# Splitting the second convolution's weights in the second stage, slab by slab, with ACT and GpSimd instead of VectorE

## The reference, cut to what matters

```python
def _dcnv2(x, w_off, b_off, w, b, k, pad):
    om = conv(x, w_off) + b_off                 # offsets and a gate for each tap of each pixel
    sy, sx = offsets + pixel grid + tap grid
    mask = sigmoid(om[:, 2 * P:])
    val = _bilinear(x, sy, sx) * mask           # four neighbours, weighted
    return einsum('ncphw,ocp->nohw', val, w) + b

h = _bn_lrelu(_dcnv2(x, w_off1, b_off1, w1, b1, 1, 0), ...)   # 512 -> 256 channels, 1 tap
h = _bn_lrelu(_dcnv2(h, w_off2, b_off2, w2, b2, 3, 1), ...)   # 256 -> 512 channels, 9 taps
return x + h
```

## Time and profile before

| | us |
|---|---|
| median of 3 runs | 3176.06 (3172.43 to 3177.47) |
| the profiled execution | 3181.72 |
| its span on the core | 3179.9 |
| mean granted TensorE clock | 0.984 of full speed |

### The profile page before, as it was taken

The page is one execution under the profiler, slowest core; times in us unless marked ns, Lnnn a source line. Parts: engine busy times, 40 slices in busy tenths (PEclk is TensorE's granted clock), DMA queues, the critical chain, the costliest instruction groups (busy, mean ns, idle before and its releaser), DMA issues.

```text
span 3179.9 us, 52201 instructions
## 1 busy us (share of the span) xinstructions
PE 3045.7 (96%) x15660; PEld 2472.5 (78%) x15660; DVE 2755.8 (87%) x4830; ACT 2510.6 (79%) x4736; POOL 1681.7 (53%) x1701
## 2 busy tenths in 40 slices
PE   6997888989999999999999999999999999999998
PEld 6997445558888888888888888888888888888888
DVE  5545899978999998998999998999989999999987
ACT  3665677778888888888888888888888888888886
POOL 0001444456656666566566666566666665666652
PEclk8999899989999999999999999999999999999999
DMA  8998999999999999999999999999999999999994
GB/s 310 322 339 299 352 349 332 334 332 398 373 357 378 368 362 376 365 365 379 359 370 377 357 372 374 356 381 367 359 379 363 364 368 350 362 362 352 367 347 174
DMA packets 432939, 1124.82 MB, mean 354 GB/s; under 512 B 42908, under 2 KB 173084, under 8 KB 432848
## 3 DMA queue, kind: packets, MB, share of 16 engines
q0 software_dynamic: 244672, 891.09, 75.1%
q1 hardware_dynamic: 116944, 161.19, 14.4%
q10 hardware_dynamic: 71232, 71.57, 6.5%
HBM read 1003.70 MB, written 137.04 MB: 359 GB/s over the span
## 4 chain that ended last, share of the span: by engine, by line
PE 69%; DVE 17%; issue 6%; ACT 5%; DMA 2%; ACTq 1%; DVEq 0%; SPq 0%; POOLq 0%
PE psum_t L1269 49%; PE psum_t L1256 9%; PE psum_t L386 5%; PE psum_t L697 4%; DVE arena L1190 4%; DVE val_first L1198 2%; DVE z_sb L1212 2%; DVE val_lo L1205 2%; DVE arena L835 1%; ACT val_hi L1153 1%; ACT psum_t L1139 1%; DMA arena<-w 1%; ACT z_sb L1162 1%; PE psum_t L682 1%; DVE arena L859 1%
## 5 line engine op out<-in xcount | busy, mean ns | idle before, releaser
L1125 POOL DMA_INDIRECT arena<-table,plan_in x1521 | 1516.2, 997 | 968.6 <-DVE arena L1198 419.0
L1269 PE MATMUL psum_t<-val_hi,w_hi 128*128 128x512 f32 (+2 forms) x3096 | 1240.4, 401 | 1.8 <-ACT z_sb L1162 0.5
L1269 PE MATMUL psum_t<-val_hi,w_lo 128*128 128x512 f32 (+2 forms) x3096 | 1200.2, 388 | 0.0
L1269 PE MATMUL psum_t<-val_lo,w_hi 128*128 128x512 f32 (+2 forms) x3096 | 1196.8, 387 | 0.0
L1139 ACT ACTIVATE psum_t<-arena,plan_in 128x512 f32<-128x512 f32 x1521 | 1044.1, 686 | 138.2 <-DVE arena L1190 133.9
L1190 DVE SCALAR_TENSOR_TENSOR arena<-arena,plan_in,psum_t 128x512 f32<-128x512 f32 x1521 | 1123.1, 738 | 10.6 <-ACT psum_t L1139 10.5
L1269 PEld LDWEIGHTS psum_t<-val_hi,w_hi 128*128 128x128 f32 x3096 | 582.6, 188 | 137.2 <-ACT z_sb L1162 36.2
L1269 PEld LDWEIGHTS psum_t<-val_hi,w_lo 128*128 128x128 f32 x3096 | 581.7, 188 | 121.1
L1205 DVE TENSOR_TENSOR val_lo<-psum_t,val_hi 128x1024 fp32r<-128x1024 f32 (+2 forms) x387 | 465.4, 1203 | 230.4 <-ACT val_hi L1153 230.3
L1269 PEld LDWEIGHTS psum_t<-val_lo,w_hi 128*128 128x128 f32 x3096 | 583.7, 189 | 102.9
L1153 ACT ACTIVATE val_hi<-psum_t 128x1024 fp32r<-128x1024 f32 (+2 forms) x387 | 390.0, 1008 | 281.2 <-PE psum_t L1256 281.0
(11 more groups left out here) (90 smaller groups left out, 2454.7 us busy)
## 6 DMA issues: line engine op xcount, KB each, us to landing
arena<-x SPq DMA_DIRECT2D x90, 512.0 KB, 8.3
table<-arena ACTq DMA_DIRECT2D x42, 896.0 KB, 8.3
out<-arena SPq DMA_DIRECT2D x136, 256.0 KB, 4.7
table<-arena ACTq DMA_DIRECT2D x42, 768.0 KB, 7.1
arena<-x SPq DMA_DIRECT2D x70, 384.0 KB, 6.3
arena<-table,plan_in POOLq DMA_INDIRECT x1521, 6.7
table<-table SPq DMA_DIRECT2D x32, 512.0 KB, 8.8
arena<-w POOLq DMA_DIRECT2D x2, 2304.0 KB, 13.9
```

The lines of the kernel that those rows point to most:

```text
L1125: nc.gpsimd.indirect_dma_start(landing(r, i)[:, :], None, rows, bass.IndirectOffsetOnAxis(ap=row.bitcast(u32), axis=0))\
L1269: last = nc.tensor.matmul(psum_acc[:, oc, 0:n], a[:, w, oc * P:(oc + 1) * P], b[:, r % 2, kt, 0:n], start=(w == 0 and a is w2_hi and b is ...
```

## The change

1. The two DMAs of nine slabs, the wait between them, and `split_w2` leave the first stage. DVE's program there is `lower` for every tile, and the plan.
2. A new buffer `w2_slab` of 128 x 512 holds one raw slab. In the second stage SP loads two slabs at the start of its step of chunks 0 to 8, each after the split of the slab before it.
3. ACT makes the high part of slab 2c in its step of tile 13c + 19, and of slab 2c + 1 in that of tile 13c + 25, after the folds.
4. POOL makes the low part nine tiles later in its own order, before the gather of tile 13c + 28 or 13c + 34. It waits for ACT's high part.
5. POOL no longer waits for the slabs before its first gather. PE waits for all of them at the second stage's end.

```diff
+SPLIT_AT = (19, 25)
+SPLIT_LAG = 9
...
-                pool.wait_ge(w1_scaled, 1)
-                for part_no in range(2):
-                    if part_no:
-                        pool.wait_ge(w2_split, HALF_SLABS)
-                    pool.dma_start(w2_raw, w2[part_no * HALF_SLABS * P:(part_no + 1) * HALF_SLABS * P, :]
-                                   .rearrange("(s p) n -> p s n", p=P)).then_inc(raw_loaded[part_no], 16)
...
-                    if s == 0:
-                        dve.wait_ge(raw_loaded[part_no], 16)
-                    hi, lo = w2_hi[:, slab, :], w2_lo[:, slab, :]
-                    link(nc.vector.tensor_copy(hi, w2_raw[:, s, :]))
-                    nc.vector.tensor_tensor(lo, w2_raw[:, s, :], hi.bitcast(f32), ALU.subtract)\
-                        .then_inc(w2_split, 1)
...
                 for c in range(CHUNKS):
                     n = plan_tiles(c)
+                    for slab in slabs_of(c):
+                        if slab:
+                            sp.wait_ge(w2_split, slab)
+                        sp.dma_start(w2_slab[:, :], w2[slab * P:(slab + 1) * P, :]).then_inc(w2_loaded, 16)
                     sp.wait_ge(chain2, (c + 1) * (CHAIN + 1))
...
-                pool.wait_ge(w2_split, SLABS)
+                def lower_w2(slab):
+                    pool.wait_ge(w2_hi_ready, slab + 1)
+                    nc.gpsimd.tensor_tensor(w2_lo[:, slab, :], w2_slab[:, :], w2_hi[:, slab, :].bitcast(f32),
+                                            ALU.subtract).then_inc(w2_split, 1)
+
                 pool.wait_ge(chain1, PLAN_STEPS_1)
                 for t in range(TILES):
+                    if split_at(t - SPLIT_LAG) is not None:
+                        lower_w2(split_at(t - SPLIT_LAG))
...
                 pe.wait_ge(gate_ready, CHUNKS)
+                pe.wait_ge(w2_split, SLABS)
...
+                def upper_w2(slab):
+                    act.wait_ge(w2_loaded, (slab + 1) * 16)
+                    nc.scalar.activation(w2_hi[:, slab, :], w2_slab[:, :], ACT.Identity).then_inc(w2_hi_ready, 1)
...
                     for dy in range(3):
                         if t - 7 - dy in BAND_AT:
                             fold_band(BAND_AT[t - 7 - dy], dy)
+                    if split_at(t) is not None:
+                        upper_w2(split_at(t))
```

34 lines of the change are left out of this document (16 added, 18 removed).

## The result

| | before, us | changed, us |
|---|---|---|
| median of 11 runs | 3174.05 (3171.65 to 3179.53) | 3183.2 (3180.85 to 3187.49) |
| the profiled execution | 3181.72 | 3185.43 |
| its span | 3179.9 | 3183.6 |

The changed kernel takes 1.0027 times as long, with an interval of 1.0019 to 1.0036: 9.1 us slower. That is within the range, and on the other side of the forecast, which was 1.1 us faster. Two rivals had a sum near it: "full lock" +8.8 (3184.9 us) and "the first stage gives less" +7.4 (3183.5 us).

The account below looks back on a forecast made before the run. The prediction took TensorE to bound the first stage and VectorE the second. Its terms, -16.5 + 5.5 + 9.9 + 0 = -1.1 us, put on 3176.06, gave 3175.0 us, with a range of 3163 to 3186.

Parts of the forecast that it names:

- full lock: Rival, second stage: every GpSimd subtraction holds VectorE for its rest, 19.8 us; sum +8.8, 3184.9 us; chance 0.15.
- the first stage gives less: Rival, first stage: transfers bound it, so the gain is about 8 us instead of 16.5; 3183.5 us; chance 0.10.
- Step 1: First stage: slab loads and splits leave, TensorE's two gaps go; -16.5 us, ends 15 and 18.
- Step 2: Second stage: high part on ScalarE delays `near` at j = 6, nine times 0.61; +5.5 us, ends 0 and 6.
- Step 3: Second stage: low part on GpSimd disturbs VectorE by 0.55 us per slab; +9.9 us, ends 0 and 20.
- Step 4: Second stage: slab loads on SP land in time; 0 us, ends 0 and 4 over nine chunks.

Follow-up runs that it names:

- the slabs loaded early: Changed kernel with four places for raw slabs, each slab loaded a chunk ahead, GpSimd still subtracting: second stage 367.2 us, ratio to the kernel before 1.0019.
- the later slabs: Kernel before with VectorE's slab splits moved one chunk on in the first stage; three runs: second stage 347.8, 351.0 and 351.3 us, ratios 0.9997, 0.9973 and 0.9976.
- second run: Kernel before and changed kernel, each unaltered and run again: second stages 351.7 and 368.8 us, changed over before 1.0054.
- the high part alone: Changed kernel with slabs loaded a chunk ahead and GpSimd only overwriting each slab, low parts left out: second stage 351.9 us, ratio to the kernel before 0.9979.
- the copy: As the high part alone, but GpSimd copies each raw slab onto itself in place of overwriting it: second stage 349.4 us, 5.3 us held.
- the overwriting: Changed kernel with GpSimd's memset of the raw slab in place of its subtraction, low parts left out: second stage 359.9 us; also used in the high part alone, 351.9 us.

## Why the prediction was wrong

The step that failed is the third, the low part on GpSimd. It said that no row lay nearer to 0 than to 1.1 us for each slab, and took the middle, 0.55. The runs put it at the upper end: 1.09 us held for each slab, 19.6 in all. With the slabs loaded early, where 22.1 us are held, the stage pays 15.3 or more. With that alone put right the sum is +4.3 and not -1.1: slower, and on the side that was measured. Step 1, which gave 4.1 us less than forecast, is nearly as large an error and lies on the same side.

- **Step 1, the first stage: right in mechanism, too large.** TensorE waits 8.1 us less from 20 to 80 us, and the later slabs show that moving VectorE's waits for slabs away gains by itself. The size was to be 16.5 us with ends of 15 and 18; it was 14.5 at tile 47 and 11.9 at the end of the stage (12.4 between the means: 307.9 over the two runs of the kernel before, 295.5 over the eight kernels that load no slab in the first stage, which lie from 294.6 to 297.2). Two parts of the term were off. The count of 54 tiles compared tile 6 with tile 60, which are two places apart in their chunks, j = 6 and j = 8. In the changed kernel, without any slab, tiles 6 and 8 start at 24.36 and 30.22, 5.86 us apart and not 2 x 1.55. So 2.8 of the 17.2 us were none of the slabs'. Of these 1.1 are the pattern of every chunk (tiles 58 and 60 start at 106.51 and 110.73, 4.22 us apart); the rest is the first gap, of which 1.86 us stay:

```profile
30.97 0.39 PE L381 MATMUL psum_t<-w_hi,val_hi 128*128 128x260 f32 x1 [1.86 <-DVE val_lo L487]
```

  There ScalarE is late by itself, with a table write that takes it 2.78 us to issue at 26.73. It stood in the trace of before behind the wait for the slab, and so the prediction gave the whole gap to the slab. The text said "a us or so" for the pattern and left the value above it. The same j in the trace of before would have taken off the 1.1. The remaining 2.7 us are lost at the stage's end: the lead is 14.6 us at tile 125 (225.89 and 211.28) and 11.9 at the last tile (301.45 and 289.58). The first gather starts 14.7 us earlier, at 256.87 in place of 271.57, but ScalarE then loses time around the last table writes:

```profile
278.09 0.63 ACT L398 ACTIVATE val_hi<-arena 128x512 fp32r<-128x512 f32 x1 [3.72 <-issue]
281.56 0.38 ACT L406 ACTIVATE arena<-psum_t 128x256 f32<-128x256 f32 x1 [2.84 <-DMA table<-arena]
```

  The kernel before had such waits as well (2.46 us for a table write at 295.84). In its second run the changed kernel has 2.8 us of waits there without a cause in the profile, and its lead over the kernel before beside it goes from 12.8 at tile 125 to 11.3. That the loss comes from there is read from the trace and wasn't tried.
- **Step 2, the high part: too dear.** Forecast 5.5 us; the high part alone and the copy give 351.9 and 349.4 against 350.0, so between -0.6 and +1.9, which single runs can't tell from nothing. The `add_far` of j = 8 is 0.46 us late in the changed kernel and 0.45 in the high part alone, where it had been 0.21. That is 0.25 more and not the 0.61 of the forecast. In the high part alone it is the only wait of its chunk, where the kernel before had three, of 0.31, 0.45 and 0.21. The other `near` are no longer late, and the chunk is 0.66 us shorter than before (26.60 against 27.26). The step charged ScalarE's whole duration to one wait and took the others as fixed; the sum of a chunk's waits fell from 0.97 to 0.45.
- **Step 3, the low part: the failing one.** It took half of the full hold. Its parts were right: L654 takes 1.276 us where 1.3 was taken (by luck, as the middle of bounds of 0.69 and 1.9), and 1.1 us for each slab was the upper end; measured, 19.6 / 18 = 1.09. What was wrong was the weight between the ends. The row that spoke for zero, `add_lower` at 466 to 490 ns beside the gathers, shows GpSimd issuing transfers, and that said nothing on a subtraction: as the runs show, an instruction of GpSimd that only writes holds nothing either (502 ns at most), and one that reads does. "No row is nearer" was true, and the middle of a range between two mechanisms is a value that neither gives: with the lock it is 1.1, without it 0. The Trainium skill, "SBUF — State Buffer", section "Who interferes with whom", has the rule: two SBUF inputs on VectorE against a GpSimd instruction that reads SBUF, and none against one that only writes. These two agree with the runs: up to 2045 ns for L866 beside the subtraction, its usual 0.75 us for the `add_far` inside one, and none held beside the overwriting. The further point, that whoever comes first holds the port, doesn't show in the records: eight of the held `add_lower` started 0.27 to 0.47 us ahead of the subtraction's recorded start, and were held all the same. In the stage it costs 15.3 us with the slabs early, by the lengths of undisturbed chunks 2.57 for a chunk.
- **Step 4, the loads: within its ends, on the dear side.** Forecast 0, ends 0 and 4. Three slabs late in the changed kernel and three again in its second run, 6.4 and 4.7 us of ScalarE's time; on the stage 3.6 and 1.6 against the loads a chunk ahead. But the place was the wrong one. The step called the second slab of a chunk close ("that is close", 8.4 us of time) and gave the first 10 us. In the changed kernel every second slab landed 2.0 to 5.1 us before it was wanted, and the late ones are slabs 2, 4 and 12, each the first of its chunk; in the second run they are slabs 2, 4 and 10. They took 10.1, 9.6 and 8.3 us from issue to landing, where 8.1 had been taken, and were wanted 8.3, 5.4 and 8.0 us after their issue, where 10 had been taken. The worst, slab 4, is issued only at 389.27, behind SyncE's loads of the plan at 386.37, which the step left out:

```profile
386.37 2.85 SPq L289 DMA_DIRECT2D plan_in<-plan  x2
389.27 11.97 SPq L633 DMA_DIRECT2D w_slab<-w  x2
```

  The step's last sentence has a slip as well: 0.5 MB in 27.3 us on top of 329 GB/s is some 348, over the 344 that it names.

The sum by what was measured: -12.4 for the first stage, between -0.6 and 1.9 for the high part, 15.3 for the low part, 1.6 to 3.6 for the loads. That is between 3.9 and 8.4, against 9.1 measured with an interval of 6.0 to 11.4 (0.0019 and 0.0036 of 3174). How the two middle terms divide depends on the disturbed run of the high part alone. By the undisturbed chunks they are -0.66 and +2.57 us a chunk, together 1.9, some 17 us for nine chunks, where the sum has 14.7 to 17.2. The signs of three terms held, and the errors of step 1 and step 3, 4.1 and 5.4 us, lie on the same side; step 2's, 4 to 6 us, lies on the other.

"Full lock" had the mechanism of step 3 right, and its sum of +8.8 is so near to 9.1 by luck: its first stage is 4.1 us too large and its high part 4 to 6 us too dear, and these errors cancel. The last rival, that the first stage gives less, gave nearly the right time (3183.5) by luck too: by it the first stage gives 8 us and the second costs 15.4, and measured they are 12.4 and some 21. It wanted transfers to bind. The later slabs, with the same transfers, lose VectorE's waits but get the gap at 85 us, so transfers do have a part in that stage, though not in the changed kernel, whose slabs come later.

One thing stays open. The spans of the two profiled executions differ by 3.7 us, the medians by 9.1. The profiled execution of before lay above every one of the 11 timed runs of that kernel. ScalarE stood there in the second stage for nothing that the profile shows (total us, times, longest):

```profile
ACT psum_t L739 <- issue: 5.9, 2, 4.4
```

Its second stage of 355.5 us is 4 us over that in its second run, which had such waits too, 7.9 us of them. So they don't account for the difference by themselves, and what does wasn't found. The prediction put its sum on the median and not on that execution, so the 5.66 us don't touch it.

## What to carry to other kernels

Before giving GpSimd work that reads SBUF, look at what the busiest engine runs at that moment: if it is VectorE with two SBUF inputs, each GpSimd instruction is paid in VectorE's time, and doing the work on VectorE itself can be cheaper (by 10.3 us for 18 slabs here). A wait for data that has not landed is first mended by asking later or loading sooner on the same engine, before the work is moved into a stage that has less room. When a stage's length is disturbed from run to run, compare the length of its repeating part. Where two mechanisms give two values for a cost, forecast one of them and give the other a chance; the mean belongs to neither.

## What the runs showed of the hardware

- A subtraction of 128x512 on GpSimd, float32 to float32r, takes 1.276 us (1.269 to 1.289); a copy 0.62, or 0.74 where an `add_lower` had started 0.45 us ahead of it; a write of constants 0.54. VectorE subtracts the same in 0.69.
- A VectorE instruction that meets the subtraction is held up to 1.55 us, longer than the 1.28 us that it is recorded for, and it was held although it started 0.46 us ahead of the subtraction's recorded start. All of them end 1.56 to 1.58 us after that start. One that ended 0.20 us ahead of it took its usual 0.48 us. The copy holds for only 0.30 us on average.
- An instruction with one of its operands in PSUM isn't held: two `add_far` lie wholly inside a subtraction and take 0.75 us, as ever, where each `add_lower` or `activate` that met one was held, except the `add_lower` behind each of these two, which began in the subtraction's last 0.1 us. No run changes the place of the operand alone.
- A load of 256 KB takes 4.8 us at best, 6.6 in the median, 10.1 at worst in the second stage, and 13.8 for the one issued at the end of the first.
- The third stage, which is the same in all these kernels, took 2515 us in the result and 243 to 308 us more on three chips later, at a lower rate of transfers. From 1100 to 1500 us, the kernel before in the result and the later slabs in their first run (columns as above):

```profile
1100.00:1500.00 400.00, 395.62 (x1965) 325.72 (x1964) 365.20 (x607) 335.22 (x582) 245.55 (x246) 1.00 0.98 367
```

```profile
1100.00:1500.00 400.00, 371.10 (x1764) 300.99 (x1763) 327.51 (x547) 299.80 (x521) 220.90 (x223) 0.97 0.92 329
```
